# Two attention layers over 16 images: values in delayed pairs, and position products of all heads in one place

## What is computed

```python
x = x + L0(gn(x))
x = x + L1(gn(x))

# L0: global attention with positions
qkv = x @ w_qkv.T + b_qkv
rel_h = einsum('bhwc,hkc->bhwk', r_q, Rh)
rel_w = einsum('bhwc,wkc->bhwk', r_q, Rw)
scores = q @ k.T * SCALE + rel_h[..., :, None] + rel_w[..., None, :]
out = softmax(scores) @ v ; out @ w_proj.T + b_proj

# L1: 7 x 7 neighbourhood attention, 16 registers as keys for all
scores = where(mask, q @ k_cat.T * scale, -1e30)
out = softmax(scores) @ v_cat ; out @ out_w.T + out_b
```

## Time and profile before

| | us |
|---|---|
| median of three runs | 4896.54 (4892.41 to 4898.04) |
| the profiled execution | 4902.5 |
| its span, first to last instruction | 4900.8 |
| main0 of one pass, 96 steps | 152.15 |
| main1 of the same pass, 102 steps | 82.77 |

### The profile page before, as it was taken

How to read it: one execution, slowest core, us unless ns; L and a number is a source line. 1 busy time by engine, 2 the same in 40 slices (tenths; PEclk the granted TensorE clock), 3 DMA queues, 4 the chain that set the end, 5 groups by cost and what they waited for, 6 DMA issues and landing times.

```text
span 4900.8 us, 97559 instructions
## 1 busy us (share of the span) xinstructions
PE 4491.2 (92%) x32598; PEld 2291.5 (47%) x32598; DVE 3079.3 (63%) x5558; ACT 2608.5 (53%) x3955; POOL 892.5 (18%) x1901
## 2 busy tenths in 40 slices
PE   5879999999999999999999999999999999999998
PEld 3334453544535454453544535455454544535444
DVE  3736667665675656667566675656657566676654
ACT  1533556555564555556555564555646555565564
POOL 3112111222202212121212202212021121102111
PEclk7888999999999999999999999999999999999999
DMA  6334242443414433253433424433144432424401
GB/s 126 83 73 86 49 104 62 99 90 70 89 39 106 87 87 71 53 108 70 99 79 70 88 52 99 94 73 84 44 106 81 99 79 48 101 62 99 87 14 40
DMA packets 235869, 386.05 MB, mean 79 GB/s; under 512 B 58396, under 2 KB 133728, under 8 KB 235360
## 3 DMA queue, kind: packets, MB, share of 16 engines
q1 hardware_dynamic: 189280, 266.13, 23.8%
q10 hardware_dynamic: 21504, 75.51, 7.6%
q0 software_dynamic: 24576, 37.80, 4.8%
HBM read 227.79 MB, written 88.08 MB: 64 GB/s over the span
## 4 chain that ended last, share of the span: by engine, by line
PE 75%; DVE 9%; SPq 5%; issue 5%; DMA 5%; ACT 2%; DVEq 0%; ACTq 0%; POOL 0%
PE P L1135 15%; PE P L1153 14%; PE P L1094 13%; PE P L958 6%; PE P L959 6%; DVE mx L901 5%; PE P L1071 5%; PE P L1185 4%; PE P L1206 4%; PE P L1102 3%; DMA QA<-queries 2%; PE P L1178 1%; SPq L507 1%; DMA biases<-xn 1%; DVE mxc L907 1%
## 5 line engine op out<-in xcount | busy, mean ns | idle before, releaser
L901 DVE TENSOR_REDUCE mx<-P 128x1 f32<-128x512 f32 x3072 | 1923.2, 682 | 471.2 <-PE P L1094 467.9
L771 ACT ACTIVATE probs<-P 128x1024 f32<-128x1024 f32 x1536 | 1507.5, 1022 | 777.7 <-PE P L1153 777.0
L1094 PE MATMUL P<-K,AR 96*128 96x256 f16 x6144 | 1093.1, 282 | 42.9 <-DMA AR<-biases 26.7
L1153 PE MATMUL P<-AR,K 113*128 113x512 f16 x3072 | 924.8, 383 | 14.1 <-DMA AR<-mrow 13.6
L907 DVE TENSOR_REDUCE mxc<-P 128x1 f32<-128x336 f32 (+1 forms) x1536 | 648.2, 474 | 307.6 <-PE P L1103 304.0
L787 ACT ACTIVATE probs<-P 128x320 f32<-128x320 f32 (+3 forms) x1632 | 618.1, 436 | 405.2 <-PE P L1206 340.0
L1135 PE MATMUL P<-probs,V 128*17 128x512 f32 x6144 | 817.2, 604 | 9.9 <-ACT probs L771 9.9
L1094 PEld LDWEIGHTS P<-K,AR 96*128 96x128 f16 x6144 | 541.7, 99 | 566.9 <-DVE mx L901 198.3
L1153 PEld LDWEIGHTS P<-AR,K 113*128 113x128 f16 x3072 | 216.9, 98 | 676.6 <-ACT probs L771 517.8
L1206 PE MATMUL P<-A,K 113*128 113x320 f16 (+2 forms) x1536 | 447.1, 306 | 12.9 <-ACT probs L787 12.1
L1102 PE MATMUL P<-K,A 112*128 112x320 f16 (+1 forms) x1536 | 400.4, 295 | 53.4 <-DVE mx L901 35.8
(11 more groups left out here) (122 smaller groups left out, 3705.4 us busy)
## 6 DMA issues: line engine op xcount, KB each, us to landing
AR<-biases SPq DMA_DIRECT2D x384, 256.0 KB, 7.7
AR<-queries ACTq DMA_DIRECT2D x96, 512.0 KB, 5.8
biases<-xn SPq DMA_DIRECT2D x192, 256.0 KB, 2.9
AR<-queries ACTq DMA_DIRECT2D x96, 256.0 KB, 8.5
K<-oraw POOLq DMA_DIRECT2D x384, 64.0 KB, 4.8
xin<-in_x_dram SPq DMA_DIRECT2D x16, 768.0 KB, 10.5
queries<-oraw SPq DMA_DIRECT2D x384, 32.0 KB, 4.8
QA<-queries SPq DMA_DIRECT2D x192, 64.0 KB, 5.1
```

What stands on the lines that cost most here:

```text
L771: nc.scalar.activation(probs[:, u % RING, j:j + 2, :], P[:, b:b + 2, :], ACT.Exp).then_inc(p_done[0], 1)
L901: V_.reduce_max(mx[:, n // 2, n % 2:n % 2 + 1], bank, AX.X).then_inc(used, 1)
L1094: last = mm(bank[:, QD * (v % 2):QD * (v % 2) + QD], AR[0:ROWS_MAX[0], part % SLOTS, v, c, j, 128 * q:128 * q + 128], K0[0:ROWS_MAX[0], h, ...
L1153: last = mm(P[:, j, :], K0[0:ROWS, h, 128 * kt:128 * kt + 128], AR[0:ROWS, p % SLOTS, kt // 2, :, j, :], start=True, stop=True)
```

## The change

1. **Values in pairs.** In main0 `use` no longer stands behind each unit. `values_due` puts two units behind every fourth step (units 0 and 1 behind step 4), up to step 88, and single ones at the end. So that ScalarE has where to write meanwhile, half units go round five half slots: the four of `probs` and `fifth`, which is part of xres. xres is therefore loaded behind step 90 instead of 32, and ScalarE waits at the start of main0 for the store of xres. In main1 `probs` is cut into three units, and values come in pairs by `values_due_local`.
2. **Position products of all twelve heads.** Sixteen jobs of four matmuls with 192 columns take the place of three times four jobs of sixteen with 64. QA holds all three groups. The results are staged in oraw, xn and xin; ScalarE's next copy into oraw waits for their stores (`rel_moved`). All sixteen stand in main1, steps 6 to 26; those of group 2 stood in main0.
3. **Order of moves.** Stores and loads go by table, not by group; QA is loaded wholly in prep.
4. **Order of max jobs.** Eleven of layer 0's part 1 move from main1 to main0, and 18 of layer 1's part 2 to the end of main0. What is left in main1 goes behind steps 0 to 5 and 28 to 37, and layer 0's from step 39.

```diff
-RELS = 4
+RELS = 16
...
-RING = 2
+PACKED = 1280, 1408, 1408
+FIFTHS = 85
+RELOAD = 90
+SECOND, THIRD = 22, 18
...
+def values_due(step):
+
+    if step % 4 == 0 and 4 <= step < FIFTHS + 4:
+        return [step // 2 - 2, step // 2 - 1]
+    if step % 2 and step > FIFTHS + 4:
+        return [step // 2 - 1]
+    return []
...
+def slot_of(step):
+
+    return step % 5 if step < FIFTHS else (step - FIFTHS) % 4
...
+def left_by(step):
+
+    return step - 5 if step < FIFTHS + 4 else step - 4
...
+def values_due_local(g, u, j):
+
+    if j:
+        return []
+    if u == 0:
+        return [(g - 1, 7), (g - 1, 8)] if g else []
+    return {2: [(g, 0)], 3: [(g, 1), (g, 2)], 5: [(g, 3), (g, 4)], 7: [(g, 5), (g, 6)]}.get(u, [])
...
-        placed = evenly(max_jobs(0, image, 2), 0, 20)
+        placed = evenly(max_jobs(0, image, 1)[SECOND:], 0, 6) + evenly(max_jobs(0, image, 2), 6, 23)
...
-    placed += [(8 + n, job) for n, job in enumerate(rel_jobs(image, 2))]
-    placed += [(16 * p - 33, ask(image, p)) for p in (3, 4, 5)] + [(16 * p - 32, fill(image, p)) for p in (3, 4, 5)]
+    for p in (3, 4, 5):
+        placed += [(16 * p - 33, ask(image, p))] + [(16 * p - 32, job) for job in fills(image, (p,))]
...
-        placed += evenly(max_jobs(1, i1, 0), 13, 32) + evenly(max_jobs(1, i1, 1), 77, 94)
+        placed += evenly(max_jobs(1, i1, 0), 15, 34) + evenly(max_jobs(1, i1, 1), 75, 87)
+        placed += evenly(max_jobs(1, i1, 2)[:THIRD], 87, 95)
...
-    placed = evenly(max_jobs(1, image, 2), 0, 25)
-    placed += [(2 + n, job) for n, job in enumerate(rel_jobs(n0, 0))]
-    placed += [(0, ask(n0, 0)), (5, fill(n0, 0)), (6, ask(n0, 1)), (6, fill(n0, 1))]
-    placed += [(24 + n, job) for n, job in enumerate(rel_jobs(n0, 1))]
-    placed += [(28, ask(n0, 2)), (28, fill(n0, 2))]
-    placed += evenly(max_jobs(0, n0, 0) + max_jobs(0, n0, 1), 25, STEPS[1] - TAIL)
+        return plan(STEPS[1], evenly(third, 5, 60) + last)
+    rel = rel_jobs(n0)
+    placed = evenly(third[:8], 0, 6) + evenly(third[8:], 28, 38)
+    placed += evenly(rel, 6, 27) + [(0, ask(n0, 0)), (6, ask(n0, 1)), (28, ask(n0, 2))]
+    placed += [(19, fill(n0, p, 0)) for p in range(SLOTS)] + [(28, fill(n0, p, 1)) for p in range(SLOTS)]
+    placed += evenly(max_jobs(0, n0, 0) + max_jobs(0, n0, 1)[:SECOND], 39, STEPS[1] - TAIL)
     return plan(STEPS[1], placed + last)
 
 
 def first_phases(image, *more):
 
...
-    first = max_jobs(0, image, 0)
-    return in_turn(*[ask(image, p) for p in range(SLOTS)], *rel_jobs(image, 0), fill(image, 0), fill(image, 1),
-                   *first[:20], *rel_jobs(image, 1), fill(image, 2), *first[20:], *more)
+    rel = rel_jobs(image)
+    return in_turn(*[ask(image, p) for p in range(SLOTS)], *rel[:10], *[fill(image, p, 0) for p in range(SLOTS)],
+                   *rel[10:], *[fill(image, p, 1) for p in range(SLOTS)], *max_jobs(0, image, 0), *more)
...
+        fifth = xres[:].rearrange("p t c -> p (t c)")[:, 0:2 * 512].rearrange("p (j n) -> p j n", j=2)
+        packed = probs[:].rearrange("p a j n -> p (a j n)")
...
-        QA = sb("QA", [128, 2, GH, QD], F16)
-        relhi, rello = (xn[:, n, :].bitcast(F16).rearrange("p (k h q) -> p k h q", k=2, h=GH) for n in range(2))
+        QA = sb("QA", [128, G, GH, QD], F16)
+        staged = (flat[:, 0:G * S // 2], xn[:].rearrange("p a n -> p (a n)")[:, 0:G * S // 2])
+        relhi = [t.bitcast(F16).rearrange("p (m q) -> p m q", q=QD) for t in staged]
+        staged = (flat[:, G * S // 2:G * S], xin[:].rearrange("p t c -> p (t c)"))
+        rello = [t.bitcast(F16).rearrange("p (m q) -> p m q", q=QD) for t in staged]
...
+        def half_unit(step):
+
+            slot = slot_of(step)
+            return fifth if slot == 4 else probs[:, slot // 2, 2 * (slot % 2):2 * (slot % 2) + 2, :]
...
-            def biases_away(im, g):
+            def biases_away(im, table):
 
                 for s, (t, ready) in enumerate(((relhi, relhi_done), (rello, rello_done))):
-                    sp.wait_ge(ready, (im * G + g + 1) * RELS)
-                    for table in range(2):
+                    sp.wait_ge(ready, im * RELS + 8 * table + 8)
+                    for g in range(G):
...
-            def fill_slot(im, p):
+                                     t[table][:, GH * g:GH * g + GH, :]).then_inc(biases_out[table], 16)
+
+            def fill_slot(im, p, table):
 
                 g, half = p // 2, p % 2
-                if p >= SLOTS:
...
-                    if g == 1:
-                        query_blocks(im, 0)
+                    if g:
+                        query_blocks(im, g - 1)
...
+                query_blocks(im, G - 1)
...
-                    fill_slot(image, part)
-                    if part in (0, 2):
-                        query_blocks(image, part // 2 + 1)
-                    if part == 1 and is_image(image, 0):
+                    fill_slot(image, part, n)
+                    if part == SLOTS - 1 and n and is_image(image, 0):
                         static_rows()
-                if what == "rel" and n == RELS - 1:
-                    biases_away(image, part)
+                if what == "rel" and n % 8 == 7:
+                    biases_away(image, n // 8)
...
+                    if kind == "main" and L == 0 and step == RELOAD:
+                        sp.wait_ge(pv_done[0], im * UNITS[0] + FIFTHS // 2 + 1)
...
+                        if not (isinstance(im, int) and im + 2 >= B):
+                            sp.wait_ge(biases_out[1], (im + 3) * PER_BIASES)
...
+                while staged_rel:
+                    image = staged_rel.pop()
+                    for table in range(2):
+                        act.wait_ge(biases_out[table], (image + 1) * PER_BIASES)
...
+                        act.wait_ge(mid_out, spilled)
...
-                        if j == 0 and u >= RING:
-                            act.wait_ge(pv_done[0], im * UNITS[0] + u - RING + 1)
+                        if left_by(step) >= 0:
+                            act.wait_ge(pv_done[0], im * UNITS[0] + left_by(step) // 2 + 1)
...
+                rel_moved()
...
-                    if n == 0:
-                        pe.wait_ge(qa_in[part], (image + 1) * PER_QA)
-                        if part:
-                            pe.wait_ge(biases_out[part - 1], (image + 1) * PER_BIASES)
-                    q = QA[:, part % 2, :, :].rearrange("p h (l w) -> p h l w", w=16)
-                    table = n // 2
-                    for b in range(8):
-                        line = 8 * (n % 2) + b
+                    for g in range(G if n == 0 else 0):
+                        pe.wait_ge(qa_in[g], (image + 1) * PER_QA)
+                    q = QA[:].rearrange("p g h (l w) -> p (g h) l w", w=16)
+                    table = n // 8
+                    for b in range(2):
+                        line = 2 * (n % 8) + b
                         rhs = q[:, :, :, line] if table else q[:, :, line, :]
                         for s in range(2):
                             lhs = Z[:, table, s, 15 - line:47 - line, :].rearrange("p x a -> p (x a)")
-                            last = mm(bank[:, 64 * b:64 * b + 64], lhs, rhs, start=(s == 0), stop=(s == 1))
+                            last = mm(bank[:, 16 * NH * b:16 * NH * b + 16 * NH], lhs, rhs,
+                                      start=(s == 0), stop=(s == 1))
                     last.then_inc(rel_done, 1)
                     return
                 if n == 0 and layer == 0:
...
-                    if u == 2 * TT - 1:
-                        pe.wait_ge(biases_out[2], (im + 1) * PER_BIASES)
...
-                    if u:
-                        use(u - 1)
+                        for due in values_due(step):
+                            use(due)
...
+                        for dg, du in values_due_local(g, u, j):
+                            use(dg * (TT + 1) + du)
...
-                    if full:
-                        use(full - 1)
+                use(UNITS[1] - 2)
```

118 lines of the change are left out of this document (65 added, 53 removed).

## The result

The changed kernel takes **5446.36 us** (median of 4 runs, 5442.79 to 5453.35) against 4895.58 us (4892.41 to 4898.04) for the kernel before: a ratio of 1.1127, 95% interval 1.1108 to 1.1146. The profiled execution has a span of 5451.6 us, 550.8 more than before. The forecast was 5430.

What follows compares the result with a forecast made beforehand. TensorE (92% busy) was taken to set the time, but not alone: VectorE's maxima wait on three banks. Fourteen passes of 11 + 24.3 us give 494, +536 with the parts around the loop: 5430 us, range 5090 to 5600.

Steps and rivals of the forecast that it cites:

- Main0, forecast 163: Main0 goes from 152.2 to 163 us, +11 a pass, with pairs and moved maxima; bounds -4 and +17.
- The mechanism and the cycle: Main0: VectorE idles 1.3 us behind a pair; four steps with eight maxima take 6.26 us against 5.84, 0.42 slower.
- rival A: The gap comes, but main0 gains 4.4 us and the rest waits less: +18 a pass, 5190 us; chance 0.17.
- the 0.20 us of the switch: TensorE saves 0.20 us a pair by fewer tiling changes: 0.11 at its end, 0.09 at its start.
- QA, forecast a wait of 21 us: Main1, step 6: the first position job waits for all of QA, about 21 us (15 to 25), before 2.5.
- From the wait to step 28, forecast 29: Main1: 23.1 us of work at full clock, plus 6 for 12 us at 1.2 GHz: 29 us.
- rival B: The gap is 25 us and the clock stays at 1.2 GHz through table 1: +44 a pass, 5600; chance 0.12.
- Steps 28 to 38, forecast 13.3: Main1: 25 layer 1 maxima, 10.8 us; ACT's copy waits for table stores (landing 2.9), making scores 2.5 us late.
- Step 39 to the end, forecast 40.2: Main1's tail takes 40.2 us as before, VectorE being nearly full, so pairs save nothing.
- Position products at 0 by the column: 192 products of 64 columns become 64 of 192; cost goes by the column, so wider ones save 0.
- rival D: Position products cost by their number, so wider ones give back 9.4 us a pass: 5290; chance 0.09.
- C: Rival: QA is there at step 6, waits go and pairs gain 6.6, 13 us a pass faster: 4705; chance 0.06.

Runs made afterwards that it cites:

- e1: The changed kernel with values one unit at a time again, in main0 and main1, all else kept: 5276.11 us, ratio 1.0772.
- e2: The changed kernel, pairs kept, each layer 0 maximum over 256 of 512 columns, query weights times 0.01: 5067.28 us, one run.
- e3: The changed kernel with the same halved layer 0 maxima and query weights times 0.01, but values one unit at a time: 5077.36 us, one run.
- e5: The changed kernel with QA loaded for image 0 alone, so later images wait for no QA load: 5240.96 us, one run.
- e7: The changed kernel with ACT's last load of queries into AR (phase 2) at step 45 of main1 instead of 28: 5362.69 us.
- e10: The changed kernel with table 1's position products over contiguous columns of QA instead of columns 32 bytes apart: 5399.95 us, one run.
- e12: The kernel before with pairs of values in main1 alone, main0, position jobs and maxima places as before: 4969.71 us, ratio 1.0141.
- e6: The changed kernel where ACT, before its first copy into oraw in main1, waits for table 0's stores alone: 5446.82 us.
- e11: The kernel before with QA part 1 loaded sooner and ACT's AR loads for phases 1 and 2 moved to steps 34 and 45: 4873.29 us, ratio 0.9954.
- e8: The kernel before with QA part 1 loaded behind the stores of queries, ahead of the first table's stores: 4940.37 us, ratio 1.0096.

## Why the prediction was right

**Main0, forecast 163, measured 162.8.** The mechanism and the cycle held: 6.16 us for four steps against 6.26 forecast, a gap of 1.30 against 1.3, 1.70 against the 1.9 beside layer 1, 0.32 lost a pair against 0.42. Over the fourteen passes it is 164.4 against 153.2 before, +11.2 where +11 was forecast. e1 shows that 5.0 of the 10.6 us of the pass shown are the pairs, so the other 5.6 are the maxima moved in. e2 and e3 show the rule behind rival A: the 0.20 us of the switch is real and is had only where VectorE does not bind. The prediction cites the Trainium skill (TensorEngine Tiling (Array Packing), Key Properties) for a drain at a change of the tiling mode; 5.46 us with a pair against 5.66 agree with it.

**QA, forecast a wait of 21 us, measured 18.3.** The chain of SyncE was laid out rightly, its last landing, 3 us, taken long: it was 1.5 (the last queries' issue ended at 2330.35, QA's began at 2331.80). What taking the wait away gives is less than the wait, though (14.5 us a pass in e5): the staging in oraw is late as well, a condition that the prediction did not name.

**From the wait to step 28, forecast 29, measured 26.5.** The slow stretch behind the wait is some 6 us long, not 12, but a second one, of some 7, comes with table 1, so its length was right for a reason only half seen. Its price of 6 us was too high: it took everything in the 12 us to go at half speed, and the products of table 1 do not. A job of theirs lasts 1.55 us at 1.00 (2346.87) and 1.57 at 0.50 (2356.22); sixteen narrow ones in the kernel before lasted 2.05 at 1.00 (2088.14) and 2.08 at 0.50. That could be read in the trace of the kernel before: the window of rows 9 holds two such jobs. What the two stretches cost is 4 us, an estimate: 3.46 us for the values over the registers, which take 1.72 at 1.00 in e1 (2298.60 to 2300.32), 2.02 instead of some 1.2 for a pair of other values, and the rest in scores and jobs of table 0. So rival B's clock came in part, and without its price. Clock windows of the changed kernel, then, of the kernel before, a job of table 1 at 0.50 and the window behind its first two (2088.14 and 2090.25):

```profile
2343.00:2347.00 4.00, 4.00 (x28) 2.33 (x27) 2.20 (x5) 3.69 (x11) 0.00 (x0) 1.00 0.00 0
...
2356.00:2358.00 2.00, 2.00 (x8) 0.90 (x7) 0.56 (x1) 1.01 (x3) 0.00 (x0) 0.50 0.98 205
```

```profile
2113.15 2.08 PE L1071 MATMUL P<-QA,Z 128*128 128x64 f16 x16
...
2090.00:2095.00 5.00, 5.00 (x25) 3.30 (x24) 1.70 (x3) 1.44 (x3) 4.61 (x9) 0.66 0.89 166
```

**Steps 28 to 38, forecast 13.3, measured 15.9.** The hold was named but sized at 2.5 us; it is 8.3. The step that failed is the landing of the stores, taken as 2.9 us although ACT's load for phase 2 is placed at the same step. e7 gives 2.9 us when it is moved. I had used this very effect for the queries of part 1 (8.0 us) and left it out for these stores. The trace of the kernel before has this case itself: 2.9 is the median over both tables' stores, and those of its second position jobs, issued beside the same load of phase 2 (2118.57), took 6.8 us from the end of their issue (2121.01) to the loads that wait for them (2127.83).

```profile
2118.47 2.54 SPq L479 DMA_DIRECT2D biases<-xn  x4
2127.83 1.72 SPq L494 DMA_DIRECT2D AR<-biases  x4
```

**Step 39 to the end, forecast 40.2, measured 44.2.** Here "pairs save nothing" was too kind: e1 gives 40.0 with singles. They cost some 2.5 us, and the low clock 1.6; the average of the fourteen is 42.8.

**Position products at 0 by the column.** The page shows 269.6 us for 1024 wide products, and 3072 narrow ones took the same 269.6; rival D is out. (So is C: TensorE waits for QA in every pass. Rival B's 5600 was some 45 us above what its own +44 a pass gives by the terms of the sum, 14 x 44 + 42 on 4896.5; nothing hangs on it.) e10 shows the cause: contiguous columns halve the line. That agrees with the rule of the Trainium skill (SBUF — State Buffer, Door 1: The DMA port swizzle) on reads that cross to a new 16-byte line.

**The sum.** In the pass shown it is +37.0 against +35.3: main0 -0.4, main1 up to the end of the wait -2.1 (by the 2107.5 that the sum takes), on to step 28 -2.5, steps 28 to 38 +2.6, the tail +3.6 (2149.8 to 2190.4 in the forecast), the out and prep stages +0.5. Over the fourteen passes it is +35.8, main0 +11.2 against 11 and main1 +24.6 against 24.3. Ahead of and behind them it was 50 us against 42. That 5430 is so near 5446 is luck in part: inside main1 errors of up to 4 us a pass cancel.

| part of the 35.8 us a pass | size | shown by |
|---|---|---|
| pairs, main0 and main1 | 10.7 | e1; e12 for main1 alone, in the kernel before, 4.4 |
| position products, and maxima moved for them | 25.1 | what is left with singles |
| of these: QA's wait | up to 14.5, with pairs | e5 |
| of these: ACT's load for phase 2 at step 28 | 6.1 | e7 |

The rows are not all apart from each other: e5 and e7 were not run together, nor were they with singles, and some 1.5 of the 10.7 are the values over the registers behind QA's wait. That the moved maxima cost 5.6 us in main0 is a difference of two stages, not a run of its own.

## What to carry to other kernels

Before two bursts on the engine that looks like the bound are joined, count how long the engine that feeds on it can live on its buffers; a gain of 0.20 us became a loss of 0.32, and halving the consumer's work showed both. When a wait is removed, look for what ends next on the same chain: e6 got nothing, e5 14.5 of 18.3 us a pass. Bulk loads that nobody waits for yet cost whoever's transfers lie beside them, and moving them was the only edit that paid in both kernels (e7 against the changed kernel, e11 against e8).

## What the runs showed of the hardware that I had not expected

- TensorE's granted clock fell while TensorE was wholly busy. In the changed kernel it is 1.00 in 2343 to 2347 and 0.50 (1.2 GHz) in 2356 to 2358, in the products of table 1 with their strided columns though TensorE is busy for the whole of both windows; with contiguous columns (e10) it is 1.00 through them. The kernel before shows the same less cleanly: 0.66 in 2090 to 2095, TensorE busy throughout, behind two such jobs, with 0.96 us of idle time ahead of them. That the stride is the cause rests on e10 alone.
- The strided products hardly notice the clock: 1.55 us a job at 1.00 and 1.57 at 0.50, and 2.05 and 2.08 in the kernel before, where sixteen contiguous ones go from 0.64 to 1.01.
- In main0, without any wait, a dip of the clock lengthens the stage: 162.8 us in one pass of the changed kernel at 1.00 and 164.4 in another with 0.91 in one stretch of 20 us, 165.3 in e7 with 0.83. The kernel before has such dips too (152.1 to 154.6 us). Effects under 2 us a pass can't be read from one stage.
- Products of 192 contiguous columns follow each other every 0.08 us with a new weight tile of 128 columns each.
- An issue on SyncE takes 0.56 to 0.9 us for 128 KB and 0.63 for 32 KB. In the changed kernel a group's queries land 1.5 to 7.8 us behind the end of their issue, with what else is in flight.
